# One core, attention and a two-expert layer: three of four pairs of context products are taken apart, the first of each between the two halves of scores

## The chip, the cores and the metric

The kernel runs on one core of a Trainium2 chip. The metric is the device time in microseconds (us), the median of several runs. TensorE (PE) multiplies matrices, VectorE (DVE) and ScalarE (ACT) work elementwise, GpSimd (POOL) does elementwise work and sends indirect DMAs, and SyncE (SP) sends the other DMAs. PEld in the profile is PE's loading of weights.

## The reference

The input x is 8 batches of 1024 rows of 128 numbers. One layer of attention and one of experts are added to it:

```python
xn = layernorm(x) * gamma + beta, cut into 8 heads of 16
q, k, v = xh @ Wq + bq, xh @ Wk + bk, xh @ Wv + bv
score = ((q + u) . k + rel_shift((q + v_bias) . p)) / sqrt(128)
x = x + softmax(score) . v @ Wo + bo
# experts: a router gives each row its two best of 8; each is
y = ((x @ W1a + b1a) * gelu(x @ W1b + b1b)) @ W2 + b2
x = x + the two y, weighted by the router
```

So there are 8 x 8 = 64 pairs of batch and head, each with scores of 1024 x 1024, and then some 16,384 rows of expert work.

## The kernel before

The program has an attention phase (the first three quarters of the time) and an expert phase. The change touches the attention phase alone, and there the order in which PE works.

Attention takes each head twice over. The **first pass** of a head makes scores only to find each row's maximum: PE writes 18 pieces of 512 columns into three PSUM buffers pA in turn (L652, L654; two of the 18 are four small products of 128 columns, L658), and DVE reduces each piece (L1076; L1082 four times for the two special ones). The **second pass** makes the scores again with the maximum in them, transposed, in nine units u = 0 to 8 of two halves of 512 columns: PE writes half 0 and half 1 of pB (L673, L675; for u = 0 four products of 128 columns each, L679), and ACT takes the exponential of each half into a buffer prob of a ring of four (L976, L978; one of the four buffers shows as b_all). PE may write a half again when ACT has read it. POOL then masks 128 x 128 of the block on the diagonal (L563 to L570). First-pass work is two heads ahead of second-pass work, so in each unit PE does one half of scores, one piece of the first pass, the other half, another piece.

The **context** of a block kb (L691) is prob times the values: `pC[32*strip : 32*strip+17]` gets 17 columns of weights (16 values and a 1 for the sum) times 256 columns of prob, for four strips of 256 columns. Each strip writes 32 partitions of its own of pC, and so uses a quarter of the array's columns; each is recorded as two matmuls, so that one context is eight records. The eight contexts of a head stand as four pairs, after the unit's second piece: in u = 1 blocks 6 and 7 of the head before, in u = 4 blocks 0 and 1, in u = 6 blocks 2 and 3, in u = 8 blocks 4 and 5. A context waits for POOL's mask of its block; ACT may write a buffer of the ring when the context that read it is done (pv_done).

At the end of many units stand **small pieces** on PE: projections for a later batch (L615, L622, L610), transposes and the router's products (L626 to L767). Which piece stands in which unit is written out by hand (M_AT, W_AT, PROJECT_AT), with the places where ACT or DVE take the result; ACT takes its own after the unit's second exponential. The loop runs over 8 batches, 8 heads in each, and nine units in each head; all engines run in the order of their own code and wait for one another by semaphores.

Of the kernel before, what the change touches and what calls it, by code (L numbers as in the profile page):

```python
# [65 lines left out]
def batches(nc, eng, head=None):  # L66

    return nc.Fori(0, B, engines=[eng.engine], hint_back_edge=True, head_slot=None if head is None else {eng.engine: head})


def attention_phase(nc, dram, keep):

    ctx = ExitStack()
    with ctx:
# [152 lines left out]
        def w_at(b, name):  # L227

            return b * W_N + W_IDX[name]
# [2 lines left out]
        ST_N = 16 * 4 * sum(len(p) for p in PLACES.values())  # L232
        STORE_AT = {2: ("c",), 3: ("k",), 4: ("gl", "gu")}
        READY = {"c": 2, "k": 4, "gl": 7, "gu": 8}
        PAIRS_AT = {1: (-1, 6), 4: (0, 0), 6: (0, 2), 8: (0, 4)}

        FOUR, SIDE = H // 2, P // 2

# [13 lines left out]
        def piece(n):  # L252

            qb, k0 = n // HPB, (n % HPB) * HALF
            return qb, k0, min(max(P * (qb + 1) - k0, 0), HALF)
# [337 lines left out]
        def _(pe):  # L593
# [4 lines left out]
            def project(nb, j, part=0, parts=1):  # L598

                first = nb == 0 if isinstance(nb, int) else False  # L600
                dst = (pE, *pA)[j % 4] if first else pE
                if j == 0:
                    pe.wait_ge(ln, (nb + 1) * LN_N)
                if part == 0 and not first:
                    pe.wait_ge(e_done, nb * E_N + (E_AT[j - 1] if j else 0))
                elif part == 0 and j >= 2:
                    pe.wait_ge(e_done, E_AT[max(j - 4, j % 2 + (2 if j >= 4 else 0))])
                if j < 2:
                    for t in range(4):
                        mm = pe.transpose(dst[:, P * t:P * t + P], xn[:, 4 * j + t, :], ident[:, :])  # L610
                else:
                    w, src = ((w_q, xnT), (w_p, qv), (w_k, xnT))[j // 2 - 1]
                    lo, hi = HALF * part // parts, HALF * (part + 1) // parts
                    at = HALF * (j % 2)
                    mm = pe.matmul(dst[:, lo:hi], w[:, :], src[:, at + lo:at + hi], start=True, stop=True)  # L615
                if part == parts - 1:
                    mm.then_inc(e_ready, 1)

            def upper_form(half, dst, part=0, parts=1):
                lo, hi = HALF * part // parts, HALF * (part + 1) // parts  # L620
                c = HALF * half + 1
                return pe.matmul(dst[:, lo:hi], to_upper[:, :], g_lo[:, c + lo:c + hi], start=True, stop=True)  # L622
# [16 lines left out]
            def first_pass(b, h, n):  # L639

                s = h % SLOTS
                if n == 0:
                    pe.wait_ge(stk[s], b * (2 * STK) + (h // SLOTS + 1) * STK)
                if not (isinstance(b, int) and h == 0 and n < S1_BUFS):
                    pe.wait_ge(s1_read, b * (H * S1U) + h * S1U + n - S1_BUFS + 1)
                dst = pA[n % S1_BUFS]
                n = ORDER[n]
                if n < NB * HPB:
                    qb, k0, low = piece(n)
                    q = slice(P * qb, P * qb + P)  # L650
                    if low > 0:
                        mm = pe.matmul(dst[:, 0:low], QL[0:KROWS, s, q], K[0:KROWS, s, k0:k0 + low], start=True, stop=True)  # L652
                    if low < HALF:
                        mm = pe.matmul(dst[:, low:HALF], QU[0:KROWS, s, q], K[0:KROWS, s, k0 + low:k0 + HALF], start=True, stop=True)  # L654
                else:
                    for i in range(4):
                        q = slice(P * (4 * (n % 2) + i), P * (4 * (n % 2) + i) + P)
                        mm = pe.matmul(dst[:, P * i:P * i + P], QU[0:KROWS, s, q], K[0:KROWS, s, q], start=True, stop=True)  # L658
                mm.then_inc(s1_ready, 1)

            def second_pass(b, h, u, half):

                s = h % SLOTS
                if u == 0 and half == 0:
                    pe.wait_ge(mrow_in[h % 2], b * (H * 16) + (h // 2 + 1) * 32)
                pe.wait_ge(p_exp, HPB * (b * (H * S2U) + h * S2U + u) + half + 1)
                r, q0 = MROW + 1, HALF * half
                if u > 0:
                    kb = u - 1
                    k = slice(P * kb, P * kb + P)  # L670
                    up = min(max(P * kb - q0, 0), HALF)
                    if up > 0:
                        mm = pe.matmul(pB[:, q0:q0 + up], K[0:r, s, k], QU[0:r, s, q0:q0 + up], start=True, stop=True)  # L673
                    if up < HALF:
                        mm = pe.matmul(pB[:, q0 + up:q0 + HALF], K[0:r, s, k], QL[0:r, s, q0 + up:q0 + HALF], start=True, stop=True)  # L675
                else:
                    for k0 in range(q0, q0 + HALF, P):
                        k = slice(k0, k0 + P)
                        mm = pe.matmul(pB[:, k], K[0:r, s, k], QU[0:r, s, k], start=True, stop=True)  # L679
                mm.then_inc(s2_ready, 1)  # L680

            def context(b, h, kb):

                quarter = S // STRIPS
                pe.wait_ge(p_mask, b * (H * NB) + h * NB + kb + 1 + LATE)
                if kb == 0:
                    pe.wait_ge(ctx_evac, b * H + h + 1)
                if kb == 0 and h in (0, H // 2):
                    pe.wait_ge(placed, b * 2 + (1 if h == 0 else 2))
                for strip in range(STRIPS):  # L690
                    mm = pe.matmul(pC[VW * strip:VW * strip + D + 1, :], vext[:, kb, h % H, :], prob[kb % RING][:, quarter * strip:quarter * strip + quarter],  # L691
                                   start=(kb == 0), stop=(kb == NB - 1), skip_group_check=True)
                mm.then_inc(pv_done, 1)
# [118 lines left out]
            with batches(nc, pe, 0) as b:  # L812
                for h in range(H):
                    for u in range(S2U):
                        second_pass(b, h, u, 0)
                        first_pass(b, h + AHEAD, 2 * u)
                        second_pass(b, h, u, 1)
                        first_pass(b, h + AHEAD, 2 * u + 1)
                        if u in PAIRS_AT:
                            back, kb = PAIRS_AT[u]  # L820
                            context(b, h + back, kb)
                            context(b, h + back, kb + 1)
                        for name, places in (*M_AT.items(), *W_AT.items()):
                            if (h, u) in places:
                                small_piece(b, name, places.index((h, u)), len(places))
                        for j, places in PROJECT_AT.items():
                            if (h, u) in places:
                                if (j, places.index((h, u))) == (6, 0):
                                    pe.wait_ge(w_done, w_at(b, "context 0") + 1)
                                if j == 0:  # L830
                                    pe.wait_ge(w_done, w_at(b, "super") + 1)
                                project(b + (2 if j < EARLY else 1), j, places.index((h, u)), len(places))
                        for half, places in enumerate(UPPER_AT):
                            if (h, u) == places[0]:
                                if half == 0:
                                    pe.wait_ge(e_done, (b + 1) * E_N + E_N)
                                    pe.wait_ge(pos, (b + 1) * POS_N + 6)
                                else:
                                    pe.wait_ge(low_done, (b + 1) * LOW_N + SPLITS.index(("gu", 0)) + 1)
                                upper_form(half, pE, 0, 2)  # L840
                            if (h, u) == places[1]:
                                upper_form(half, pE, 1, 2).then_inc(upper, 1)
# [938 lines left out]
```

## Time and profile before

| | |
|---|---|
| median of 3 runs | 1661.58 us (1659.19 to 1663.43) |
| the profiled execution's own time | 1674.05 us |
| its span, first to last instruction | 1672.3 us |
| attention's main loop | its contexts run from about 82 to 1225 us of the span |
| expert phase | from about 1310 us to the end |
| busy: PE, DVE, ACT, POOL | 92%, 84%, 66%, 64% |

Busy shares are of the whole span. The ends of matmuls are modelled and matmuls overlap, so PE's share does not say that it works at its peak: the starts of its instructions do. PEclk is the clock that TensorE was granted, as a share of 2.4 GHz.

### The profile page before, as it was taken

The page shows a single profiled execution, that of the slowest core. Times are in us where ns is not written, and L with a number is a line of the kernel's source. Part 1 is how long each engine was busy: PE and PEld are TensorE (multiplying, and loading weights), DVE is VectorE, ACT ScalarE, POOL GpSimd, SP SyncE. Part 2 cuts the span into 40 slices and gives each one's busy share as a digit, 9 for nine tenths or more (in the row PEclk, how much of TensorE's full clock was granted, in tenths as well). Part 3 has the DMA queues.
Part 4 walks back from the last instruction along what each step waited for, and adds up shares of the span by engine and source line. Part 5 has one row for each costly group of instructions (what it writes and reads, how often), then busy time and mean ns, then how long its engine had stood idle before and what let it go on. Part 6 is the DMA issues. An engine that isn't in the chain of part 4 may idle for free. (4 is left out here: it accounts for less than half of the span.)

```text
span 1672.3 us, 50620 instructions
## 1 busy us (share of the span) xinstructions
PE 1542.2 (92%) x12352; PEld 1191.0 (71%) x12353; DVE 1402.5 (84%) x5273; ACT 1109.8 (66%) x2296; POOL 1075.0 (64%) x2031
## 2 busy tenths in 40 slices
PE   4799999999999999999999999999951699999997
PEld 2476676677767767767766776776641699999997
DVE  6799799879979988998998999899854588887886
ACT  3167677766767777677777777767730577777775
POOL 3277567757756766776676677677663277666665
PEclk8699899989989999999999999999975799999999
DMA  6836355534634554464364455446443144444443
GB/s 164 238 94 200 85 133 163 143 83 117 194 91 130 160 144 115 107 188 109 106 192 131 110 159 158 107 107 204 108 154 111 39 58 57 53 56 53 55 54 48
DMA packets 133844, 199.72 MB, mean 119 GB/s; under 512 B 20888, under 2 KB 95016, under 8 KB 133632
## 3 DMA queue, kind: packets, MB, share of 16 engines
q1 hardware_dynamic: 108064, 177.07, 39.1%
q0 software_dynamic: 25568, 20.14, 8.3%
q8 instruction: 94, 1.54, 0.4%
q14 instruction: 118, 0.97, 0.2%
HBM read 108.10 MB, written 75.20 MB: 110 GB/s over the span
## 5 line engine op out<-in xcount | busy, mean ns | idle before, releaser
L1076 DVE CUSTOM_DVE_ANT_0 junk<-pA,lmask 128x512 bf16<-128x512 f32 x1056 | 686.3, 683 | 68.3 <-PE pA L654 46.9
L976 ACT ACTIVATE prob<-pB 128x512 f32<-128x512 f32 x384 | 229.9, 599 | 191.7 <-PE pB L673 110.0
L1591 POOL DMA_INDIRECT out<-yb,dst x142 | 230.3, 1622 | 130.7 <-ACT yb L1669 77.0
L652 PE MATMUL pA<-K,QL 96*128 96x512 f32 (+3 forms) x792 | 283.6, 359 | 14.8 <-DMA K<-split_operands 11.5
L675 PE MATMUL pB<-QL,K 97*128 97x512 f32 (+3 forms) x768 | 286.6, 373 | 1.4 <-ACT upper_diag L976 1.4
L673 PE MATMUL pB<-QU,K 97*128 97x512 f32 (+3 forms) x640 | 270.3, 422 | 0.6
L978 ACT ACTIVATE prob<-pB 128x512 f32<-128x512 f32 x384 | 228.1, 594 | 15.6 <-PE pB L675 6.8
L654 PE MATMUL pA<-K,QU 96*128 96x512 f32 (+3 forms) x660 | 233.4, 354 | 2.0 <-DVE acc L1076 0.6
L691 PE MATMUL pC<-prob,vext 128*17 128x256 f32 x3088 | 220.4, 389 | 0.1
L570 POOL TENSOR_TENSOR prob<-prob,upper_diag 128x128 f32<-128x128 f32 x384 | 182.9, 476 | 32.1
L673 PEld LDWEIGHTS pB<-QU,K 97*128 97x128 f32 x640 | 122.8, 192 | 107.4 <-issue 62.6
L511 POOL DMA_INDIRECT routed_rows<-sent,sent_to x144 | 156.6, 1088 | 28.6 <-issue 24.8
L563 POOL MEMSET prob<- 1x1 f32 x384 | 34.3, 89 | 216.5 <-ACT prob L978 214.3
L652 PEld LDWEIGHTS pA<-K,QL 96*128 96x128 f32 x792 | 154.7, 195 | 24.6 <-issue 12.0
L675 PEld LDWEIGHTS pB<-QL,K 97*128 97x128 f32 x768 | 148.0, 193 | 15.1 <-ACT upper_diag L976 3.3
L1082 DVE CUSTOM_DVE_ANT_0 junk<-pA,umask 128x128 bf16<-128x128 f32 x528 | 122.4, 285 | 41.5 <-PE pA L658 40.9
L1712 DVE SCALAR_TENSOR_TENSOR g<-pLin,b_all,gl 128x256 f32<-128x256 f32 x288 | 125.9, 478 | 22.6 <-PE pLin L1614 14.9
L654 PEld LDWEIGHTS pA<-K,QU 96*128 96x128 f32 x660 | 128.4, 195 | 19.3 <-DVE acc L1076 11.9
L691 PEld LDWEIGHTS pC<-prob,vext 128*17 128x17 f32 x3088 | 78.6, 98 | 86.0 <-issue 25.5
L1620 PE MATMUL pY<-w_all,g 128*128 x1136 | 138.4, 275 | 0.0
L1620 PEld LDWEIGHTS pY<-w_all,g 128*128 128x128 f32 x1136 | 133.1, 192 | 0.0
L1662 ACT ACTIVATE gl<-pGate,b_all 128x256 f32<-128x256 f32 x288 | 119.3, 464 | 13.3 <-PE pGate L1614 11.4
(308 smaller groups left out, 3576.3 us busy)
## 6 DMA issues: line engine op xcount, KB each, us to landing
QL<-split_operands SPq DMA_DIRECT2D x67, 256.0 KB, 3.6
QU<-split_operands SPq DMA_DIRECT2D x67, 256.0 KB, 4.2
K<-split_operands SPq DMA_DIRECT2D x67, 256.0 KB, 4.6
xg<-routed_rows SPq DMA_DIRECT2D x75, 132.0 KB, 2.7
split_operands<-c_h SPq DMA_DIRECT2D x36, 256.0 KB, 5.8
split_operands<-c_l SPq DMA_DIRECT2D x36, 256.0 KB, 6.1
QL<-split_operands SPq DMA_DIRECT2D x67, 128.0 KB, 3.5
QU<-split_operands SPq DMA_DIRECT2D x67, 128.0 KB, 4.1
```

What stands on the lines that cost most here:

```text
L511: po.indirect_dma_start(dram["xs"], bass.IndirectOffsetOnAxis(sent_to[:, t, j:j + 1], 0), sent[:, t, :], None).then_inc(scattered, 16)
L570: po.tensor_tensor(p, p, upper_diag[h % 2][:, P * kb:P * kb + P], ALU.add).then_inc(p_mask, 1)
L652: mm = pe.matmul(dst[:, 0:low], QL[0:KROWS, s, q], K[0:KROWS, s, k0:k0 + low], start=True, stop=True)
L654: mm = pe.matmul(dst[:, low:HALF], QU[0:KROWS, s, q], K[0:KROWS, s, k0 + low:k0 + HALF], start=True, stop=True)
L673: mm = pe.matmul(pB[:, q0:q0 + up], K[0:r, s, k], QU[0:r, s, q0:q0 + up], start=True, stop=True)
L675: mm = pe.matmul(pB[:, q0 + up:q0 + HALF], K[0:r, s, k], QL[0:r, s, q0 + up:q0 + HALF], start=True, stop=True)
L691: mm = pe.matmul(pC[VW * strip:VW * strip + D + 1, :], vext[:, kb, h % H, :], prob[kb % RING][:, quarter * strip:quarter * strip + quarter ...
L976: act.activation(p[:, 0:HALF], pB[:, 0:HALF], ACT.Exp, scale=SCALE).then_inc(p_exp, 1)
L978: act.activation(p[:, HALF:S], pB[:, HALF:S], ACT.Exp, scale=SCALE).then_inc(p_exp, 1)
L1076: v.tensor_tensor_reduce(out, src[:, :], lmask[:, at:at + HALF], 1.0, -3.0e38, ALU.add, ALU.max, acc[:, s, qb, n % 2:n % 2 + 1]).then_inc( ...
L1591: po.indirect_dma_start(dram["out"], bass.IndirectOffsetOnAxis(dst[k][:, a:a + 1], 0), yb[k][:, a, :], None, compute_op=ALU.add).then_inc( ...
L1620: mm = pe.matmul(pY[k % 2][:, a, :], g[k % 2][:, c, P * a:P * a + P], keep["w2"][:, bass.ds(ex * F + c * E, E)], start=(c == 0), stop=(c = ...
```

## The change

In the units 1, 6 and 8 the first context of the pair moves from the unit's end to its middle, behind the first piece of the first pass and ahead of the second half of scores. The second context stays where it was, and so does the pair of unit 4. No instruction is added or removed, and no other engine's order changes.

```diff
-        PAIRS_AT = {1: (-1, 6), 4: (0, 0), 6: (0, 2), 8: (0, 4)}
+        PAIRS_AT, APART_AT = {1: (-1, 6), 4: (0, 0), 6: (0, 2), 8: (0, 4)}, (1, 6, 8)
...
                         second_pass(b, h, u, 0)
                         first_pass(b, h + AHEAD, 2 * u)
+                        if u in APART_AT:
+                            back, kb = PAIRS_AT[u]
+                            context(b, h + back, kb)
                         second_pass(b, h, u, 1)
                         first_pass(b, h + AHEAD, 2 * u + 1)
                         if u in PAIRS_AT:
                             back, kb = PAIRS_AT[u]
-                            context(b, h + back, kb)
+                            if u not in APART_AT:
+                                context(b, h + back, kb)
                             context(b, h + back, kb + 1)
```

## Rows read from the trace of the kernel before

**Rows 1.** Windows: length, busy PE, PEld, DVE, ACT, POOL, granted clock, DMA share, GB/s.
```profile
614.00:1176.20 562.20, 554.57 (x4566) 393.67 (x4564) 516.27 (x2117) 415.52 (x841) 392.79 (x905) 1.00 0.50 137
```
**Rows 2.** PE's timeline, one head, units 6 to 8: start, length, operation, count.
```profile
725.05 0.56 PE L658 MATMUL pA<-K,QU 96*128 96x128 f32 x4
725.45 0.28 PE L673 MATMUL pB<-QU,K 97*128 97x128 f32 x1
...
725.91 0.28 PE L654 MATMUL pA<-K,QU 96*128 96x256 f32 x1
726.12 1.06 PE L691 MATMUL pC<-prob,vext 128*17 128x256 f32 x16
727.10 0.50 PE L673 MATMUL pB<-QU,K 97*128 97x512 f32 x1
727.45 0.40 PE L652 MATMUL pA<-K,QL 96*128 96x512 f32 x1
...
729.28 0.34 PE L673 MATMUL pB<-QU,K 97*128 97x384 f32 x1
...
729.51 0.44 PE L652 MATMUL pA<-K,QL 96*128 96x512 f32 x1
729.89 0.63 PE L691 MATMUL pC<-b_all,vext 128*17 128x256 f32 x8
730.33 0.61 PE L691 MATMUL pC<-prob,vext 128*17 128x256 f32 x8
730.87 0.66 PE L679 MATMUL pB<-QU,K 97*128 97x128 f32 x4
731.37 0.28 PE L652 MATMUL pA<-K,QL 96*128 96x128 f32 x1
```
**Rows 3.** PE's instructions by line and shape from 614 to 1176 us.
```profile
L636 PE MATMUL pM<-ident_f,ctxp 128*128 128x128 f32 x56 | 10.7, 272 | 0.0
L615 PE MATMUL pE<-xnT,w_k 128*128 128x256 f32 x32 | 9.7, 385 | 0.0
```
**Rows 4.** PE's timeline in unit 3 of the same head.
```profile
718.69 0.39 PE L675 MATMUL pB<-QL,K 97*128 97x512 f32 x1
719.20 0.51 PE L654 MATMUL pA<-K,QU 96*128 96x512 f32 x1
```
**Rows 5.** PE's timeline at the router's fold (L752), fourth and eighth batch.
```profile
613.95 0.40 PE L654 MATMUL pA<-K,QU 96*128 96x512 f32 x1
615.28 0.55 PE L752 MATMUL pM<-ident_f,hr 128*128 128x128 f32 x3 [0.93 <-DVE hr L1175]
...
1176.12 0.40 PE L654 MATMUL pA<-K,QU 96*128 96x512 f32 x1
```
**Rows 6.** Waits over the span: engine, line, what for, us, times, longest.
```profile
PEld pA L654 <- DVE acc L1076: 11.9, 30, 0.8
```
**Rows 7.** ACT's timeline in unit 6 and at the start of unit 7.
```profile
725.99 0.60 ACT L978 ACTIVATE prob<-pB 128x512 f32<-128x512 f32 x1
726.48 0.59 ACT L911 ACTIVATE rp<-pM 128x512 f32<-128x512 f32 x1
726.96 0.63 ACT L898 ACTIVATE gl_h<-g_lo 128x512 fp32r<-128x512 f32 x1
727.72 0.60 ACT L976 ACTIVATE prob<-pB 128x512 f32<-128x512 f32 x1
```
**Rows 8.** PE's timeline: the piece ahead of the fold, first and second batch.
```profile
173.52 0.40 PE L654 MATMUL pA<-K,QU 96*128 96x512 f32 x1
...
320.29 0.40 PE L654 MATMUL pA<-K,QU 96*128 96x512 f32 x1
```
**Rows 9.** The window in which the granted clock first fell in the main loop.
```profile
192.60:206.20 13.60, 13.60 (x68) 9.35 (x68) 6.11 (x44) 4.70 (x9) 4.87 (x13) 0.50 0.04 12
```
**Rows 10.** PE's timeline just ahead of that window.
```profile
189.72 0.96 PE L759 MATMUL pM<-r_cols,rq 128*128 128x16 f32 x8
...
191.55 0.95 PE L626 MATMUL pE<-hsum,qv 128*128 128x8 f32 x8
```

## The prediction

> **What bounds the kernel now.** I read first the windows of the trace, for a stretch in which nothing disturbs the pattern: from 614 to 1176.2 us the granted clock is 1.00 throughout [rows 1]. By the timeline the piece ahead of the router's fold stands at 613.95 us in the fourth batch and at 1176.12 us in the eighth [rows 5], so four batches take 562.17 us, one 140.54 us, and one head 140.54 / 8 = 17.57 us. In that window PE counts as busy for 554.6 of 562.2 us, DVE for 516.3 (92%), ACT for 415.5 (74%). Modelled ends make the first of these worth little, so the second view is PE's timeline by start times [rows 2], from which I take prices per instruction:
>
> - Half of scores, or a piece of the first pass: 729.28 to 729.51 us, 0.23 us. Where it consists of four products of 128 columns: 725.05 to 725.45, 0.40 us, so 0.10 us for each 128.
> - A second context behind a first: 729.89 to 730.33, 0.44 us. Each of its two rounds of four strips of 256 columns is 0.22 us, and that is also my price for a small piece's matmul of 256 columns.
> - A pair of contexts with its way in and out: the last piece before it starts at 725.91 and needs half of 0.23, so it is through at about 726.03; the piece behind the next half of scores starts at 727.45, and that half takes 0.23, so PE was free for it at 727.22. The pair took 1.19 us. In unit 8: 729.51 + 0.23 = 729.74, and 731.37 - 0.40 = 730.97, so 1.23 us. Of this 2 x 0.44 = 0.88 us is the contexts' own streaming. The remaining 0.31 us (0.35 in unit 8) is paid once for a block of contexts, however many are in it: the first context starts 0.09 to 0.15 us after the piece before it is through (726.12 against 726.03, 729.89 against 729.74), and the rest goes on the way back to full-width work.
>
> A head of PE's work is then: 36 halves and pieces, four of them of the split kind (both halves of unit 0, and two pieces), 32 x 0.23 + 4 x 0.40 = 8.96 us; four pairs, 4 x 1.19 = 4.76 us; small pieces, of which the groups by line hold 432 matmuls of 128 or fewer columns and 128 of 256 columns in these 32 heads ([rows 3] show a group of each kind), (432 x 0.10 + 128 x 0.22) / 32 = 2.23 us. The sum is 15.95 us of 17.57. So PE is the bound, and it truly waits or is unaccounted for 1.62 us a head. DVE's 92% says that it is close behind: part of these 1.62 us is PE waiting for DVE. In unit 3 the two starts at 718.69 and 719.20 us are 0.51 apart where 0.23 would do, so PE waited 0.28 us for DVE's reduction [rows 4]. Ahead of the fold it is 613.95 to 615.28, 1.33 us less 0.23, once in a batch [rows 5].
>
> **The change part by part.** No instruction is added. Three of a head's four blocks of two contexts become two blocks of one, so four entries and exits become seven. What each step costs or gives:
>
> 1. Three more entries and exits a head, at 0.31 us: 0.93 us of PE, on PE's in-order path. 64 x 0.93 = 59.5 us. Units 6 and 8 are packed at the place where the context goes in: in unit 8 the second half starts 0.23 us before the piece that follows it and that piece is followed directly by the contexts, so there is no hole in the middle of the unit for the extra 0.31 us. The trace has no single context, so the price is bounded: not below the entry's 0.09 us plus nothing for the exit (0.09 x 192 = 17 us), not above 0.35 (67 us). I take 0.31, since both rows measure exactly this, a block against its streaming.
> 2. Waits of PE that shrink. The moved context gives DVE, between a unit's first and second piece, 0.44 + 0.31 = 0.75 us more, while the gap at the unit's end shrinks by 0.44. What DVE is late with after a lengthened unit is less late by up to 0.31 us. I count unit 3's 0.28 us once a head, and the fold, whose chain over DVE and POOL starts in unit 6 of head 4 and has the extra entries of unit 8 and of unit 1 of head 5 in it, 0.62 us a batch or 0.08 a head. That is at most 0.36 us a head; part of what DVE is late with it owes to its own order, so I take 0.30, near the upper end: 0.30 x 64 = 19 us back. The profile's own list of PE's waits for pA is small (11.9 us in 30 waits for the largest row [rows 6]), which speaks against more. From below: nothing comes back.
> 3. ACT. The second half's scores come 0.75 us later in these units, so the second exponential and what ACT does behind it do too. In unit 6 that is an evacuation and a split, until 726.96 + 0.63 = 727.59, and the next exponential starts at 727.72 [rows 7]. Moved by 0.75, that work ends at 728.34; the next unit's scores come 0.31 us later than before, so its exponential could start at 728.03. ACT is late by 0.31 us there. PE feels this only when the half after next has to wait, and unit 7 holds small pieces that cover most of it. About ten of the 24 changed units of a batch have that much on ACT behind the exponential: at most 0.31 x 10 / 8 = 0.39 us a head, 25 us; at least nothing. I take 0.05 us a head, 3 us, since the cover is seen.
> 4. Masks and the ring. Blocks 2 and 4 were masked three units before their contexts (unit 3 against 6, unit 5 against 8), and block 6 of the head before two units earlier, so asking half a unit sooner adds no wait. The buffers come free half a unit sooner; no wait of ACT for pC is among its waits, so this gives nothing. Both at 0.
>
> The sum: 59.5 - 19 + 3 = 43.5 us, on the profiled execution's own 1674.05: 1717.5 us. The median of the runs is 12.5 us lower. The likeliest reason is in the clock: the piece ahead of the fold stands at 173.52 in the first batch and 320.29 in the second [rows 8], a period of 146.77 against 140.54 us, because the granted clock was 0.50, that is 1.2 GHz, from 192.60 to 206.20 us [rows 9]. Such a fall costs 6.23 us, and two fewer of them would make 12.46 us. I put the change on the median: 1661.6 + 43.5 = 1705.
>
> The Trainium skill (TensorEngine Tiling, Key Properties) says that changing the tiling mode, not just the tile, drains TensorE. It gives no price. If the only price were the weight load that cannot be hidden behind it, by the load formula of the Trainium skill (TensorE: Matmul & The Clock Gate, LDWEIGHTS) 128 columns take about 107 ns and 17 columns 14 ns, an estimate of 0.12 us a block: by it step 1 would be 192 x 0.12 = 23 us, and not the 59.5 that the rows above give. The sum goes by the rows.
>
> **The rivals.**
>
> - *Feeding evenly wins (faster).* Scores and pieces reach ACT and DVE in a steadier stream, and PE's waits of 1.62 us a head go altogether. Then a head is 17.57 + 0.93 - 1.62 = 16.88 us, -0.69 x 64 = -44 us, 1617 us. It decides from the point where more than 0.93 of the 1.62 us vanish. For it: DVE at 92%. Against it: the waits that I can place (units 3 and the fold) lie mostly where the change reaches them with 0.31 us, and some of the 1.62 us is my rounding of prices.
> - *The new entries fill holes (no change, or little).* If PE waited in the middle of units 1, 6 and 8 for ACT's read of the other half, the context would stand in that wait. It needs 0.31 us there. In units 6 and 8 I find none: 725.45 follows the four products at 725.05 by their own 0.40 us. Taking it for unit 1 alone: 59.5 - 64 x 0.31 = 40, less 19, 21 us, so 1683; for all three units the change disappears into the bound of no difference.
> - *Nothing comes back, and ACT is late in full.* 59.5 + 25 = 84.5 us, 1746 us. For it: the two stacked pieces of unit 6. Against it: units 7 and 2 carry small pieces in most heads.
> - *The clock falls more often.* The fall at 192.60 us follows two groups of very small matmuls, eight of 16 columns and eight of 8, that each take about 0.95 us [rows 10]. It came in the first three batches and then not, with the same work. More gaps on PE can only help it to fall; in five more batches it would cost 5 x 6.23 = 31 us on top of the forecast, 1736 us. The place where it falls holds no moved context, which speaks against.
>
> **How the numbers follow.** Forecast (1683 to 1725 us): 0.70. Nothing back, ACT late or more falls (over 1725): 0.12. Mostly hidden (1667 to 1683): 0.06. Within 0.3% (1657 to 1667), which is about what a measurement of this kernel can tell from no change: 0.04. Faster: 0.08. The range 1670 to 1733 leaves out about 0.13 below and 0.06 above. It takes in the bounds of the entry's price (17 and 67 us, less and plus the others). Slower by over 0.3%: 0.88.
>
> **What the changed profile would show.** Step 1: contexts as blocks of eight records in units 1, 6 and 8, with the same 0.09 to 0.15 us ahead, and a block of one context taking 0.75 us from the end of the piece before it to the start of the half behind it; units 6 and 8 longer by 0.3 us; a batch of about 140.5 + 5.4 = 146 us where the clock is full. Step 2: the 0.51 us in unit 3 near 0.23, and the fold's 1.33 us near 0.8. Step 3: after the second exponential of unit 6 no idle time on ACT before the first of unit 7. The prediction is wrong if a block of one context costs no more than its 0.44 us of streaming and a little, if PE's waits shrink by more than an entry costs, or if the number of clock falls changes by more than two.

## The result and the profile after

The changed kernel takes 1729.98 us (median of 4, 1720.79 to 1731.75) against 1662.51 us for the one before (median of 4). The ratio is 1.0384, 95% interval 1.034 to 1.0428: 67.5 us slower by the medians, 64 by the ratio, where 43.5 were forecast. Here and below a ratio leaves out executions that took over 1.5% more than the fastest of their kernel. The profiled execution has 1731.75 us against 1674.05, 57.7 us more. Both comparisons matter below, because they differ in the clock.

The timeline of PE, changed kernel, at the two ends of a batch in which the granted clock is 1.00 throughout (the counterpart of [rows 5]):

```profile
778.18 0.40 PE L654 MATMUL pA<-K,QU 96*128 96x512 f32 x1
779.70 0.44 PE L752 MATMUL pM<-ident_f,hr 128*128 128x128 f32 x2 [1.12 <-DVE hr L1179]
...
925.58 0.40 PE L654 MATMUL pA<-K,QU 96*128 96x512 f32 x1
```

A batch takes 925.58 - 778.18 = 147.40 us, against 140.54: 6.86 us more, 0.86 us a head, 8 x 6.86 = 54.9 us in all at full clock. And the wait ahead of the fold, 778.18 to 779.70, is 1.52 us and not 1.33: it grew.

PE's timeline in unit 6 of the head shown in [rows 2]:

```profile
747.11 0.56 PE L658 MATMUL pA<-K,QU 96*128 96x128 f32 x4
747.60 0.63 PE L691 MATMUL pC<-prob,vext 128*17 128x256 f32 x8
748.15 0.33 PE L673 MATMUL pB<-QU,K 97*128 97x128 f32 x1
...
748.54 0.28 PE L652 MATMUL pA<-K,QL 96*128 96x256 f32 x1
748.66 0.28 PE L654 MATMUL pA<-K,QU 96*128 96x256 f32 x1
748.87 0.62 PE L691 MATMUL pC<-prob,vext 128*17 128x256 f32 x8
749.43 0.50 PE L673 MATMUL pB<-QU,K 97*128 97x512 f32 x1
749.77 0.40 PE L652 MATMUL pA<-K,QL 96*128 96x512 f32 x1
```

The four products are through at 747.11 + 0.40 = 747.51, the second half's scores are taken at 0.23 before the piece at 748.54, so the single context held PE from 747.51 to 748.31, 0.80 us. The second held it from 748.66 + 0.12 = 748.78 to 749.77 - 0.23 = 749.54, 0.76 us. Together 1.56 against 1.19 for the pair, 0.37 us for one more block. The step from one piece of this kind to the next, 747.11 to 749.77, is 2.66 us, against 725.05 to 727.45 = 2.40 before [rows 2]: 0.26 net. The 0.11 us between the two numbers lie in the second half's scores. PE's timeline of the kernel before, at a row between those of [rows 2]:

```profile
725.79 0.28 PE L652 MATMUL pA<-K,QL 96*128 96x256 f32 x1
```

They took 0.34 us there, 725.45 to 725.79, and not the 0.23 that I take for a half. Whether that was a hole or the pace of their first product of 128 columns (0.10 us each by [rows 2]) the rows do not say; the 0.26 net does not depend on it.

The same account for all units, from the start of one unit's scores to the start of the next one's, median of the heads at full clock: of the batch's 6.86 us, units 1 have 2.2, units 6 have 2.2 and units 8 have 2.1, which is 0.27 us for each of the 24 new blocks. All the other units together have 0.4, so on balance nothing came back there.

ACT's timeline at the same place (the counterpart of [rows 7]):

```profile
748.74 0.60 ACT L982 ACTIVATE prob<-pB 128x512 f32<-128x512 f32 x1 [0.76 <-PE pB L675]
...
749.71 0.63 ACT L902 ACTIVATE gl_h<-g_lo 128x512 fp32r<-128x512 f32 x1
750.23 0.60 ACT L980 ACTIVATE prob<-pB 128x512 f32<-128x512 f32 x1
```

No idle time stands ahead of the exponential at 750.23, as forecast; its scores are there at 749.43 + 0.50 = 749.93 and it starts 0.30 us later, where 0.31 were forecast. Unit 3 of this head (the counterpart of [rows 4]):

```profile
740.79 0.39 PE L675 MATMUL pB<-QL,K 97*128 97x512 f32 x1
741.25 0.50 PE L654 MATMUL pA<-K,QU 96*128 96x512 f32 x1
```

It is 0.46 us where 0.51 stood; only 0.05 of the 0.28 us came back. And the wait is not one of every head. The kernel before, unit 3 of the head ahead of that in [rows 4]:

```profile
701.90 0.39 PE L675 MATMUL pB<-QL,K 97*128 97x512 f32 x1
702.13 0.50 PE L654 MATMUL pA<-K,QU 96*128 96x512 f32 x1
```

The two starts are 0.23 us apart. In the eight heads of a batch they are 0.50 or 0.51 us apart in one, the one that I had read, and 0.22 to 0.26 in the other seven.

Then the clock. A fall of the changed kernel's, with the instructions just ahead of it:

```profile
330.05 0.40 PE L654 MATMUL pA<-K,QU 96*128 96x512 f32 x1
331.57 1.05 PE L752 MATMUL pM<-ident_f,hr 128*128 128x128 f32 x4 [1.12 <-DVE hr L1179]
```

```profile
331.70:338.50 6.80, 6.80 (x33) 4.52 (x34) 3.06 (x15) 3.20 (x6) 2.11 (x5) 0.50 0.92 235
```

This fall begins at 331.7 us, directly behind the fold's wait of 1.52 us; three more of the six in the main loop begin within 2 us of that wait in their batches (481.9, 1082.6 and 1232.8 us). The other two begin at 202.0 and 946.1 us, right behind the eight products of 8 columns at L626. In the kernel before, no fall stood behind the fold: all four of its main loop (192.6, 339.3, 486.1 and, for 3.4 us, 1196.1) followed those tiny products [rows 9, 10].

Over whole runs the mean granted clock tells the rest. In the changed kernel's four runs it was 0.946, 0.953, 0.945 and 0.946, with 1731.75, 1720.79, 1729.71 and 1730.25 us. Runs of the kernel before in one later job have 0.956 with 1660.25 us and 0.948 with 1674.19 us. So 0.008 of mean clock goes with 13.9 us there, and 0.007 with 11 us here: about 1.6 us for each 0.001. The usual 0.955 of before against 0.946 is then some 14 us, and 54.9 + 14 = 69 us is the 67.5 measured, within what these numbers can tell. The two profiled executions, with 0.948 and 0.946, differ by 57.7 us, near the 54.9 alone.

### The profile page after: what moved, and what is told of

Same layout as the page of the kernel before. It is cut to its first block and busy times, and to the rows that moved or that the text cites. A ratio compares the mean times of both kernels' runs of the same rounds, so it can differ in the third digit from the quotient of the medians.

```text
span 1730.0 us, 50620 instructions
## 1 busy us (share of the span) xinstructions
PE 1598.0 (92%) x12352; PEld 1175.4 (68%) x12353; DVE 1413.9 (82%) x5273; ACT 1118.0 (65%) x2296; POOL 1070.4 (62%) x2031
## 5 line engine op out<-in xcount | busy, mean ns | idle before, releaser
L1080 DVE CUSTOM_DVE_ANT_0 junk<-pA,lmask 128x512 bf16<-128x512 f32 x1056 | 695.4, 685 | 116.7 <-PE pA L654 72.3
L652 PE MATMUL pA<-K,QL 96*128 96x512 f32 (+3 forms) x792 | 285.1, 361 | 14.3 <-DMA K<-split_operands 11.7
L675 PE MATMUL pB<-QL,K 97*128 97x512 f32 (+3 forms) x768 | 292.5, 381 | 1.4 <-ACT upper_diag L980 1.4
L673 PE MATMUL pB<-QU,K 97*128 97x512 f32 (+3 forms) x640 | 280.8, 439 | 2.0 <-ACT prob L980 1.1
L691 PE MATMUL pC<-prob,vext 128*17 128x256 f32 x3088 | 245.4, 390 | 0.4 <-POOL prob L570 0.4
L570 POOL TENSOR_TENSOR prob<-prob,upper_diag 128x128 f32<-128x128 f32 x384 | 189.3, 493 | 32.0
L652 PEld LDWEIGHTS pA<-K,QL 96*128 96x128 f32 x792 | 156.0, 197 | 22.8 <-issue 12.2
L511 POOL DMA_INDIRECT routed_rows<-sent,sent_to x144 | 149.9, 1041 | 28.3 <-issue 22.6
L1709 DVE TENSOR_TENSOR w_l<-w_all,w_h 128x1024 fp32r<-128x1024 f32 x73 | 89.2, 1222 | 41.9 <-ACT w_h L1661 24.5
```

Of the source, the lines that this page charges most:

```text
L570: po.tensor_tensor(p, p, upper_diag[h % 2][:, P * kb:P * kb + P], ALU.add).then_inc(p_mask, 1)
L1080: v.tensor_tensor_reduce(out, src[:, :], lmask[:, at:at + HALF], 1.0, -3.0e38, ALU.add, ALU.max, acc[:, s, qb, n % 2:n % 2 + 1]).then_inc( ...
```

## The experiments

Each ratio is against the kernel before on the same chip, with its 95% interval; "us" is (ratio - 1) x 1662.5. A batch is from one piece ahead of the fold to the next, in a batch at full clock. The usual mean clock is the median over the executions in the ratio. Diffs are against the kernel before or the changed one, as their lines show, and shortened where `...` stands.

| kernel | ratio (interval) | us | batch at full clock | usual mean clock |
|---|---|---|---|---|
| changed | 1.0384 (1.034 to 1.0428) | +64 | 147.40 | 0.946 |
| only unit 8 apart | 1.0162 (1.0129 to 1.0195) | +27 | 142.69 | 0.947 |
| both in the middle | 1.0854 (1.0816 to 1.0891) | +142 | none whole | 0.919 |
| apart, later place | 1.0268 (1.024 to 1.0296) | +45 | 146.72 | 0.956 |
| three blocks | 1.0247 (1.0216 to 1.0278) | +41 | 143.61 | 0.942 |
| tiny, 17 columns | 1.0702 (1.0605 to 1.08) | +117 | none whole | 0.927 |
| tiny, 128 columns | 1.0515 (1.037 to 1.066) | +86 | none whole | 0.938 |
| all four apart | 1.0612 (1.0464 to 1.0759) | +102 | 149.14 | 0.943 |
| wider products | 0.9969 (0.9954 to 0.9985) | -5 | 140.61 | 0.958 |
| fold later | 1.0005 (0.9981 to 1.0029) | +1 | 140.63 | 0.955 |
| changed, fold later | 1.0369 (1.0346 to 1.0393) | +61 | 147.6 | 0.954 |
| both edits | 0.9976 (0.9966 to 0.9985) | -4 | 140.6 | 0.959 |

**Only unit 8 apart.** One of the three splits alone.

```diff
-        PAIRS_AT, APART_AT = {1: (-1, 6), ...}, (1, 6, 8)
+        PAIRS_AT, APART_AT = {1: (-1, 6), ...}, (8,)
```

> Only the pair of unit 8 is taken apart. Theory A (each extra block of contexts costs its way in and out, about 0.31 us on PE): 64 x 0.27 to 0.31 = 17 to 20 us more than before, a third of the whole change; a batch at full clock about 2.3 us longer than 140.5. Theory B (the cost is that the second half of scores and the second piece come late and leave ACT and DVE without work): unit 8 is followed by unit 0, whose scores and exponentials are the slowest to come, so more than a third, 25 us or more.

The fold's piece at full clock, PE's timeline:

```profile
1049.84 0.39 PE L654 MATMUL pA<-K,QU 96*128 96x512 f32 x1
1051.34 0.33 PE L752 MATMUL pM<-ident_f,hr 128*128 128x128 f32 x1 [1.11 <-DVE hr L1179]
...
1192.53 0.39 PE L654 MATMUL pA<-K,QU 96*128 96x512 f32 x1
```

A batch is 142.69 us, 2.15 more, 0.27 us a block and close to a third of 6.86, as theory A has it: 17 us. Unit by unit the whole of it is in units 8 (0.27 us on the mean). The measured 27 us have some 10 more, at a mean clock of 0.947. The fold's wait is 1.50 us: this one split, with no other, already makes it longer.

**Both in the middle.** The number of blocks is that of before; only the place changes.

```diff
                         first_pass(b, h + AHEAD, 2 * u)
+                        if u in APART_AT:
+                            back, kb = PAIRS_AT[u]
+                            context(b, h + back, kb)
+                            context(b, h + back, kb + 1)
                         second_pass(b, h, u, 1)
...
-                            context(b, h + back, kb + 1)
+                                context(b, h + back, kb + 1)
```

(The last line stands under `if u not in APART_AT`.)

> In units 1, 6 and 8 both contexts stand in the middle, so there are four blocks a head as before, but the second half of scores and the second piece come 1.2 us later. Theory A: the time of before, within 10 us, since no entry is added. Theory B: at least what the change costs, +60 us or more, since the delay is 1.19 us in place of 0.75. A part of theory A that I add: the pause at the unit's end is when DVE catches up, so without it PE's wait ahead of the router's fold grows from 1.33 us to 1.5 or more.

Theory A alone fails here: +142 us with no block added. ACT's and PE's timelines in unit 6 and 7 of the same head:

```profile
804.22 0.60 ACT L983 ACTIVATE prob<-pB 128x512 f32<-128x512 f32 x1 [1.19 <-PE pB L675]
...
805.19 0.63 ACT L903 ACTIVATE gl_h<-g_lo 128x512 fp32r<-128x512 f32 x1
805.71 0.59 ACT L981 ACTIVATE prob<-pB 128x512 f32<-128x512 f32 x1
```

```profile
804.26 0.40 PE L673 MATMUL pB<-QU,K 97*128 97x512 f32 x1
804.49 0.39 PE L652 MATMUL pA<-K,QL 96*128 96x512 f32 x1
804.87 0.39 PE L673 MATMUL pB<-QU,K 97*128 97x256 f32 x1
```

The scores of unit 7's first half are there at 804.66, and ACT takes them at 805.71: 1.05 us late, behind the late exponential and the two pieces that stand behind it. That is step 3 of the prediction at its full size. PE waits 0.15 us at 804.87 (804.49 + 0.23 = 804.72) for the other half. At full clock units 7 and 2, right behind units 6 and 1, take 0.38 and 0.35 us longer on the mean than in the kernel before, and units 6, 1 and 8 themselves 0.07 us or less. This profiled execution, with 1828.46 us, lies above the kernel's median of 1806.67; the rows of units 6 and 7 are from a stretch at full clock. The fold's wait is 1.72 to 1.74 us in all eight batches:

```profile
181.76 0.49 PE L654 MATMUL pA<-K,QU 96*128 96x512 f32 x1
183.49 0.47 PE L752 MATMUL pM<-ident_f,hr 128*128 128x128 f32 x1 [1.24 <-DVE hr L1180]
```

The clock fell in every batch, to a mean of 0.92 from 100 to 1200 us. By 1.6 us for each 0.001 the usual 0.919 against 0.955 is some 58 of the 142 us, an estimate.

**Apart, at a later place.** The first context stands between the second half of scores and the second piece.

```diff
-                        if u in APART_AT:
-                            back, kb = PAIRS_AT[u]
-                            context(b, h + back, kb)
                         second_pass(b, h, u, 1)
+                        if u in APART_AT:
+                            back, kb = PAIRS_AT[u]
+                            context(b, h + back, kb)
                         first_pass(b, h + AHEAD, 2 * u + 1)
```

> In units 1, 6 and 8 the first context stands behind the second half of scores and ahead of the second piece. Seven blocks a head, ACT gets its scores as early as before. Theory A: the time of the changed kernel, +55 to +65 us. Theory B with ACT as the one that starves: back to near the time of before, +20 us or less.

```profile
332.38 0.40 PE L654 MATMUL pA<-K,QU 96*128 96x512 f32 x1
333.70 0.44 PE L752 MATMUL pM<-ident_f,hr 128*128 128x128 f32 x2 [0.92 <-DVE hr L1179]
...
479.10 0.39 PE L654 MATMUL pA<-K,QU 96*128 96x512 f32 x1
```

The batch is 146.72 us, 6.18 more than before: 49 us, nine tenths of the change's 54.9. So the blocks cost nearly the same at both places. The 5.4 us between them bound ACT's lateness only roughly, since DVE's share differs too: the fold's wait, which stayed at 1.32 us here, is 8 x 0.2 = 1.6 us of them. The mean clock is 0.956, and the time is 20 us better than the changed kernel's. Neither theory had that: A expected 55 to 65 us, B 20 or less.

**Three blocks.** The computation is that of before, one block less a head.

```diff
-        PAIRS_AT = {1: (-1, 6), 4: (0, 0), 6: (0, 2), 8: (0, 4)}
+        PAIRS_AT = {1: (-1, 6, 2), 4: (0, 0, 3), 7: (0, 3, 3)}
...
+                            for i in range(n):
+                                context(b, h + back, kb + i)
```

> Eight contexts of a head in three blocks at the ends of units: blocks 6 and 7 of the head before in unit 1, 0 to 2 in unit 4, 3 to 5 in unit 7. The computation is the same. Theory A: one entry fewer a head, 64 x 0.31 = 20 us less than before, about 1642 us, unless a context now waits for POOL's mask. Theory B (spreading helps, clumping starves): slower than before by 10 us or more.

```profile
913.71 0.40 PE L654 MATMUL pA<-K,QU 96*128 96x512 f32 x1
915.34 0.33 PE L752 MATMUL pM<-ident_f,hr 128*128 128x128 f32 x1 [1.23 <-DVE hr L1175]
...
1057.32 0.40 PE L654 MATMUL pA<-K,QU 96*128 96x512 f32 x1
```

A miss for theory A: the batch is 3.07 us longer, not 2.5 shorter. An entry is saved, but a pair's 1.23 us taken out of unit 8 make it only 0.97 us shorter, and unit 0 behind it gets 0.26 us longer (medians by head at full clock, mean of the heads). That these units now run at the pace of ACT and DVE is my reading; no run tested it. The fold's wait is 1.63 us.

**A tiny matmul in the middle, a quarter wide and full width.** The kernel before, with one matmul that nothing reads, in a spare part of pC's bank; N is 17 or 128. The kernels have no other difference in their loop. These are the only two runs that put instructions into it.

```diff
                         first_pass(b, h + AHEAD, 2 * u)
+                        if u in (1, 6, 8):
+                            pe.matmul(pZ[0:N, :], ident[:, 0:N], ident[:, 0:32], start=False, stop=False, ...)
                         second_pass(b, h, u, 1)
```

> The kernel before, with one tiny matmul added in the middle of units 1, 6 and 8: 17 columns of weights and 32 columns of data, written to a spare part of pC's bank, so that it uses a quarter of the array's columns as a context does; nothing reads it. Its own streaming is about 0.03 us. Theory A (changing the way the array is cut costs 0.2 to 0.3 us): +35 to +60 us. Theory C (a context is dear because of its own eight records and weight loads, not because of the change of cut): +10 us or less.

> The same tiny matmul with 128 columns of weights, over the array's full width. Theory A: only its own issue, 192 x 2 x 0.05 to 0.1 us, +5 to +22 us, well below the run with 17 columns. Theory C: the same as the run with 17 columns or more, since its weights are longer.

Unit 6 with 17 columns, then with 128 (two recorded matmuls each, line numbers one higher):

```profile
784.19 0.56 PE L659 MATMUL pA<-K,QU 96*128 96x128 f32 x4
784.68 0.23 PE L820 MATMUL pC<-ident_f 128*17 128x32 f32 x2
...
785.25 0.29 PE L653 MATMUL pA<-K,QL 96*128 96x256 f32 x1
```

```profile
759.85 0.56 PE L659 MATMUL pA<-K,QU 96*128 96x128 f32 x4
760.24 0.36 PE L820 MATMUL pC<-ident_f 128*128 128x32 f32 x2
...
760.80 0.28 PE L653 MATMUL pA<-K,QL 96*128 96x256 f32 x1
```

From the four products to the next piece it takes 1.06 us with 17 columns, 0.95 with 128, and 725.05 to 725.79 = 0.74 without. So a product that streams for almost nothing costs 0.32 us when it is a quarter wide, as much as a block's way in and out; a full-width one costs 0.21. PE's weight loads at these places:

```profile
784.68 0.11 PEld L820 LDWEIGHTS pC<-ident_f 128*17 128x17 f32 x2
760.18 0.30 PEld L820 LDWEIGHTS pC<-ident_f 128*128 128x128 f32 x2
```

The quarter-wide product has the shorter loads and the higher price, so theory C fails: loading weights is not what makes it dear. What these two runs show of the width itself is the 0.11 us between them. The tiny products are float32 and recorded as two matmuls each, as the contexts are, between products of float32r; no run has that change alone, so how the other 0.21 us divide between it, the loads and the way in and out is open.

In whole time neither price explains +117 and +86 us: 3 x 64 x 0.32 = 61 and 3 x 64 x 0.21 = 40 us are at hand, and my upper bounds of 60 and 22 us were both passed. A part of the rest is a wait that no other kernel here has. PE's timeline, 17 columns, at the turn from one batch to the next, and the rows of PE's waits for the whole span, 17 columns and then 128:

```profile
1029.79 0.61 PE L692 MATMUL pC<-prob,vext 128*17 128x256 f32 x8
1034.94 1.11 PE L680 MATMUL pB<-QU,K 97*128 97x128 f32 x4 [4.53 <-issue]
```

```profile
PE pB L680 <- issue: 31.6, 7, 4.6
PE pB L680 <- issue: 23.5, 7, 4.2
```

Seven times, at each turn of the loop over the batches, PE stands for 4.4 to 4.6 us (2.9 to 4.2 with 128 columns), and "issue" says that the profile shows nothing that it waited for. In both kernels a fall of the clock begins during each of the seven waits or less than 1.5 us behind it (at 1032.6 us for the one shown). So these 31.6 and 23.5 us and a good part of the mean clocks of 0.927 and 0.938 belong to a side effect of the added instructions, whose cause is open, and not to the price of a visit. These two runs are read for what they show on the spot, not for their whole time. One of the four executions with 128 columns took 5746.92 us; nothing here explains it, and the ratio leaves it out.

The fold's wait here is short (180.22 to 181.35); a pause in the middle goes with a shorter wait where the pair's own pause at the unit's end stays:

```profile
180.22 0.40 PE L655 MATMUL pA<-K,QU 96*128 96x512 f32 x1
181.35 0.44 PE L753 MATMUL pM<-ident_f,hr 128*128 128x128 f32 x2 [0.74 <-DVE hr L1179]
```

**All four apart.** `APART_AT = (1, 4, 6, 8)`.

> The pair of unit 4 is taken apart too. Theory A: a further 64 x 0.27 to 0.31 = 17 to 20 us on top of the changed kernel, about +75 to +85 us over before. Theory B: less than that, since what follows unit 4 carries small pieces in every head and hides a late start.

The batch is 149.14 us, 1.74 more than the changed kernel's, 0.22 us a block and 14 us in all. The four executions took from 1749.13 to 1810.5 us. The ratio gives +102 us with an interval from 77 to 126, too wide to say more than that the expected 75 to 85 is in it.

**The kernel before again.**

> The kernel before once more, for its clock. If falls of the granted clock explain why the profiled execution was 12.5 us over the median, this one shows two or so fewer falls of 13.6 us in the main loop and a time near 1662 us, or as many falls and a time near 1674 us; a batch at full clock stays 140.5 us.

It took 1668.95 us at a mean clock of 0.951, with 34 us of its main loop at half clock (two falls of 13.7 us and two of 3.4) where the first profile had 44, and a batch of 140.5 us where the clock was full. It is a single execution. Neither of the two cases, but between them, as the clock's share would have it.

**Wider products.** The kernel before; the tiny products ahead of its falls [rows 10] are given 64 columns each by repeating their own; DVE reads the first copy. The lines are shortened.

```diff
-  (..., H*blk : H*blk+H), t2[...], hsum[:, :]
+  (..., 64*blk : 64*blk+64), t2[...], hsum[:, :].unsqueeze(1).to_broadcast([P, 8, H])
-  dst[:, 16*j : 16*j+16], gz[...], wr2
+  dst[:, 64*j : 64*j+64], gz[...], wr2.unsqueeze(1).to_broadcast([P, 4, 16])
```

> The kernel before, with the router's logits and the super-diagonal products made 64 columns wide in place of 16 and 8 (the same columns repeated; the readers take the first copy). Their weight loads set their pace already, so at full clock a batch stays near 140.5 us. Theory D (the falls of the granted clock follow these stretches of tiny matmuls): the falls in the seventh head go, 5 to 20 us less than before. Rival: the falls have nothing to do with these products, then within 3 us of before.

Windows over the main loop, of the kernel before and of this one (the column behind the engines is the granted clock):

```profile
100.00:1200.00 1100.00, 1084.95 (x8760) 767.95 (x8754) 992.21 (x4065) 799.06 (x1616) 756.85 (x1740) 0.98 0.50 136
```

```profile
100.00:1200.00 1100.00, 1085.08 (x8930) 770.34 (x8930) 1008.75 (x4151) 812.68 (x1645) 767.45 (x1771) 1.00 0.50 138
```

The eight logits products still take 1.00 us where they took 0.96, so the batch stays at 140.6 us. In its profile no fall is left in the main loop. The time is 5 us better, with the interval clear of one (2.5 to 7.6 us), at the low end of theory D's 5 to 20; the rival's 3 us or less are just inside it. Its eight runs lie within 4.3 us (1653.52 to 1657.81) where the 24 of before spread to 1683.72. It is faster than the kernel before by 0.3%, and so than the changed one.

**Fold later, before and changed, and both edits.**

```diff
-  M_AT = {..., "fold": ((5, 3),), "context 4": ((5, 5),), ...}
+  M_AT = {..., "fold": ((5, 5),), "context 4": ((5, 7),), ...}
-  ACT_OUT = {..., "fold": (5, 4), "context 4": (5, 6), ...}
+  ACT_OUT = {..., "fold": (5, 6), "context 4": (5, 8), ...}
```

> The kernel before, with the router's fold two units later (unit 5 in place of 3 of the sixth head) and context 4's transpose likewise (7 in place of 5). PE's wait of 1.33 us ahead of the fold should go: about 1.0 us a batch, 8 us in all, 1654 us. Rival: PE waits as long somewhere else, for the fold's result is wanted at a fixed place, then the time of before.

> The changed kernel with the same later fold. Theory D2 (in the changed kernel the clock falls start at the fold, where PE waits 1.52 us, and are the part of its loss that a batch at full clock does not show): 9 us of wait and some 10 us of falls go, 15 to 22 us less than the changed kernel, about 1710 us; the falls right behind the fold are gone from its clock. Rival (falls come from the extra blocks wherever they stand): only the 9 us of wait, 1721 us.

> The kernel before with both edits, wider products and later fold. If the two act apart: the sum of the two gains, 1640 to 1650 us, with hardly any fall of the clock in the main loop. Rival: taking one cause away moves the fall to the next thinnest stretch, then no better than the better of the two.

The kernel before with the later fold:

```profile
323.62 0.40 PE L652 MATMUL pA<-K,QL 96*128 96x512 f32 x1
323.85 0.60 PE L752 MATMUL pM<-ident_f,hr 128*128 128x128 f32 x4
...
464.48 0.60 PE L752 MATMUL pM<-ident_f,hr 128*128 128x128 f32 x4
```

The wait is gone, 0.23 us are left of 1.33, and the batch is 464.48 - 323.85 = 140.63 us, no shorter. The rival was right: PE waits elsewhere, with 14.0 us in 38 waits for pA at L652 where 8.1 in 23 stood. Unit by unit, unit 3 of the fold's head is 1.30 us shorter, and units 4, 5, 7 and 8 of the same head are 0.52, 0.10, 0.47 and 0.23 us longer.

In the changed kernel the ratio moves from 1.0384 to 1.0369, inside both intervals, and a batch at full clock stays at 147.6 us. Its profile has no fall behind the fold any more; the three that it has begin at 347.7, 791.4 and 1242.0 us, all right behind the tiny products of L626, where those of the kernel before stood. Its usual mean clock is 0.954, nearly that of before. By 1.6 us for each 0.001 the step from 0.946 should give 13 us; by the ratios it is 2.5 us and by the medians over before 8 (59.6 against 67.5), and the changed kernel's interval alone is 7 us to either side. So the fold's wait is where four of its falls began, and moving the fold took those away; what they cost in whole time is not settled by these runs.

The two edits together give no more than the wider products alone, as the rival had it, and their profile has no fall between 100 and 1200 us either. A single profile's falls say little, though: the kernel before with the later fold has 10 us at half clock in its main loop, where the two profiles of the kernel before have 44 and 34, and its usual time is the same within 0.3%.

## Why the prediction came out as it did

It was right in sign and in its main mechanism, and 24 us short. It lies within the stated range of 1670 to 1733 us, by 3 us; its narrower forecast of 1683 to 1725, given 0.70, was missed, and the time fell among those over 1725, given 0.12. Two errors made the sum too small, in step 2 and in the clock. One the other way, step 1's 59.5 us against some 52 measured in the changed units, hid a part of them, and that was luck.

**Step 1, the extra blocks: held.** Forecast 0.31 us each. Measured on PE's timeline 0.37 gross and 0.26 net in unit 6, 0.27 for each new block in the account of all units, 0.27 a head with unit 8 alone. At another place of the unit the blocks still cost 49 of 54.9 us. A tiny product of a context's width costs 0.32 on the spot and one of full width 0.21, so it is not the contexts' own streaming and weights that are paid again; how much of it is the change of width alone is shown only to be 0.11 us or more. The Trainium skill (TensorEngine Tiling, Key Properties) says that such a change of tiling mode drains TensorE. The runs agree that the visit has a price; a drain as such no row shows. The 0.12 us estimated from the load formula of the Trainium skill (TensorE: Matmul & The Clock Gate, LDWEIGHTS) was far too low.

**Step 2, waits that shrink: failed.** I took 0.30 us a head, 19 us, back. The first reason is in its own reading: the 0.28 us of unit 3 was counted once a head and stands in one head of eight, so that it was 0.28 us a batch and not 2.24. The second is that the fold's wait, which was to shrink by 0.62 us a batch, grew from 1.33 to 1.52 us. At full clock the batch grew by 6.86 us against 3 x 8 x 0.31 = 7.44, and in the account of all units the unchanged ones are 0.4 us a batch longer: nothing came back. The step's own sentence held a reason for the fold, that the pause at the unit's end shrinks by 0.44 us, and I gave it no weight. Across the kernels the wait follows that pause: 1.13 us with a pause added and the pair left whole, 1.33 with the pair whole or the second piece behind the first context, 1.50 and 1.52 with the second piece ahead of a single context, 1.63 and 1.73 with no contexts at the end of units 6 and 8. That it is DVE's backlog that the pause works off is an argument from this order, with DVE as the one waited for in each row; no run took DVE's work away. And the later fold shows that even a wait which vanishes is paid at another place, so crediting single waits was wrong in kind.

**Step 3, ACT's lateness: held in size.** The exponential of unit 7 has no idle time before it. It starts 0.30 us after its scores are there. At full clock unit 7 is longer in one head of eight, by 0.33 us, 2.6 us in all; forecast 3. That this one is ACT's doing is not shown. With both contexts in the middle ACT is 1.05 us late, and the units behind are longer by 0.35 us and more.

**Step 4, masks and the ring: held at nothing.** The waits of PE's weight loads for POOL's masks (L691 for L570) are 9.9 us in 28 where 12.9 in 42 stood, and no wait of ACT for pC's contexts is new.

**The clock: the missing term.** The sum had none; the rival gave 31 us for five more falls. What came is about 14 us, an estimate by the mean clocks. The profiles have four falls and six in the main loop, 44 and 48 us at half clock, which is within the two that the prediction allowed itself; that is also why the two profiled executions differ by little more than the 54.9. The remark that the falls of the kernel before came in three batches and then not holds for its profile up to 1196.1 us, where a fourth of 3.4 us stands; in its second profile they stand in other batches. With the wider products neither of two profiles has a fall between 100 and 1200 us, and nothing changed at full clock, so the tiny products take part in causing them. In the changed kernel four of six fell to the place behind the fold instead, and left it when the fold moved; why its longer wait does that, and the same wait with all four pairs apart does not (its three falls stand elsewhere), is open. It was not tried with wider products.

**The rivals.** Even feeding lost: nothing near 0.93 us a head came back. Its mirror image lost too, since clumping contexts in three blocks costs 25 us at full clock. Holes for the new entries: at most 0.11 us in unit 6, counted above. Nothing coming back, the half of the third rival, is what happened; ACT late in full, its other half, is not.

## What to carry to other kernels

Count the visits of TensorE to work of another width, not only the products: here each extra visit to quarter-wide work cost about 0.3 us, with next to no work of its own or with 0.44 us. Where such a block stands matters apart from how many there are, as two runs show: +142 us with the number of blocks unchanged, and +41 us with one block less a head. Before a wait is credited for every round of a loop, look whether it stands in every round; and a single wait that disappears is no gain until the period of the loop is shorter. A run that adds instructions as a probe can bring waits of its own: look for them before its whole time is read. Read the period at full clock and the mean granted clock apart: of this change's loss one fifth was clock by the estimate above, and with the tiny products widened, at nearly no cost, the profiled main loops had no fall.

## What was not expected of the hardware

- The granted clock fell in a loop in which TensorE counts as busy for 1084.95 of 1100 us. Eight products of 16 columns and eight of 8, each group about 0.95 us, preceded falls of 13.6 us to 1.2 GHz that cost 6.23 us each [rows 8, 9, 10]. With 64 columns each, at nearly the same pace (1.00 us for 0.96), the clock was 1.00 from 100 to 1200 us in the profiles of both kernels that have them.
- A product of 17 by 32 columns in the middle of three units of nine, 192 in all, made the kernel 7% slower. Its own 0.32 us explain 61 of the 117 us; seven waits of 4.5 us at the turns of the outer loop, each with a fall of the clock in it or right behind it, came with it.
- The same program repeats its batch to within 0.1 us at full clock (140.5 to 140.6) and its time still spreads from 1656.53 to 1683.72 us over 24 runs, with the mean clock going from 0.959 to 0.942.
